# Setup of a fused condition-and-FFN kernel on one Trainium2 core: column sums on VectorE, a large write in four parts, two transfers shared with ScalarE, and a new order

## The reference

```python
# block 0
h   = gelu(gelu(cond @ W0 + b0) @ W1 + b1)
att = softmax(h @ W2 + b2)                      # 128 samples x 8
agg_w = einsum('bk,koi->boi', att, weight)      # one 64x64 matrix per sample
agg_b = att @ bias_k
c = einsum('boi,bih->boh', agg_w, x) + agg_b[:, :, None]
x = x + c @ (A @ B.T).T + bias                  # rank 128, 1024 -> 1024
# block 1
c = conv1d(x, w, K=9, pad=4, groups=4) + (cond @ c_weight.T)[:, :, None] + fside[None, :, None]
z = einsum('nh,erh->ner', c, lora_A); top1 = argmax(c @ gate_w.T + expert_bias)
x = x + c @ W_up.T + lora_B[top1] @ z[top1]     # 1024 -> 1024
```

## Time and profile before

| | us |
|---|---|
| median of 3 runs | 1119.54 |
| range of the runs | 1117.38 to 1119.77 |
| the profiled execution's own time | 1119.37 |
| its span | 1117.6 |
| TensorE busy | 1085.9 (97%) |
| VectorE busy | 911.1 (82%) |
| ScalarE busy | 613.5 (55%) |
| mean granted TensorE clock | 0.99 |

### The profile page before, as it was taken

How to read it: one execution, slowest core, us unless ns; L and a number is a source line. 1 busy time by engine, 2 the same in 40 slices (tenths; PEclk the granted TensorE clock), 3 DMA queues, 4 the chain that set the end, 5 groups by cost and what they waited for, 6 DMA issues and landing times.

```text
span 1117.6 us, 19137 instructions
## 1 busy us (share of the span) xinstructions
PE 1085.9 (97%) x7020; PEld 1052.2 (94%) x7020; DVE 911.1 (82%) x1670; ACT 613.5 (55%) x1243; POOL 4.5 (0%) x17
## 2 busy tenths in 40 slices
PE   6599999999999999999999999999999999999998
PEld 4478999999999999999999999999999999999998
DVE  5899788888878878878888887887887887888774
ACT  5675555545555555555655555554555555555541
POOL 1000000000000000000000000000000000000000
PEclk9699999999999999999999999999999999999999
DMA  8844455554445554445554454555445555544321
GB/s 317 268 71 135 117 119 151 149 141 138 116 106 153 143 159 128 122 120 128 146 153 138 137 119 104 154 146 151 132 118 114 142 144 156 132 136 121 83 58 76
DMA packets 118048, 152.03 MB, mean 136 GB/s; under 512 B 21836, under 2 KB 91980, under 8 KB 117804
## 3 DMA queue, kind: packets, MB, share of 16 engines
q1 hardware_dynamic: 116516, 148.49, 49.4%
q10 hardware_dynamic: 1440, 2.33, 0.6%
HBM read 80.87 MB, written 35.95 MB: 105 GB/s over the span
## 4 chain that ended last, share of the span: by engine, by line
PE 91%; DVE 4%; DMA 2%; issue 1%; SPq 1%; ACT 1%; DVEq 0%; ACTq 0%
PE M L1398 41%; PE H L1398 9%; PE G L1398 9%; PE F L1347 8%; PE F L1299 7%; PE F L1269 3%; PE F L1271 3%; PE F L1270 3%; PE F L1332 2%; PE M L1332 2%; PE M L1429 2%; DMA Br<-in_Bd_dram 1%; PE F L1287 1%; PE F L1286 1%; DMA Xr<-x 1%
## 5 line engine op out<-in xcount | busy, mean ns | idle before, releaser
L1398 PE MATMUL M<-Wsh,yh 128*128 128x384 f32 x896 | 313.1, 349 | 0.4 <-DVE yl L939 0.4
L1398 PE MATMUL M<-Wsh,yl 128*128 128x384 f32 x896 | 302.9, 338 | 0.0
L1398 PE MATMUL M<-Wsl,yh 128*128 128x384 f32 x896 | 302.9, 338 | 0.0
L888 DVE STREAM_TRANSPOSE yr<-F 128x512 f32<-128x512 f32 x126 | 90.2, 716 | 128.9 <-PE F L1347 80.7
L1398 PEld LDWEIGHTS M<-Wsh,yh 128*128 128x128 f32 x896 | 168.6, 188 | 5.6 <-DVE yl L939 0.7
L1398 PEld LDWEIGHTS M<-Wsl,yh 128*128 128x128 f32 x896 | 168.9, 188 | 2.8
L1398 PEld LDWEIGHTS M<-Wsh,yl 128*128 128x128 f32 x896 | 168.2, 188 | 0.0
L438 ACT ACTIVATE yh<-yr 128x1024 fp32r<-128x1024 f32 (+1 forms) x127 | 120.2, 946 | 53.6 <-DVE yr L903 41.4
L539 ACT ACTIVATE F<-F,cbX 128x128 f32<-128x128 f32 x248 | 69.0, 341 | 94.9 <-PE F L1332 94.1
L539 ACT ACTIVATE F<-M,cbX 128x128 f32<-128x128 f32 x260 | 72.4, 342 | 66.1 <-PE M L1332 66.0
L438 ACT ACTIVATE xTh<-xTr 128x1024 fp32r<-128x1024 f32 x64 | 67.3, 1052 | 61.7 <-DMA xTr<-in_xT_dram 61.7
(11 more groups left out here) (206 smaller groups left out, 2478.0 us busy)
## 6 DMA issues: line engine op xcount, KB each, us to landing
x<-in_xP_dram SPq DMA_DIRECT2D x64, 516.0 KB, 4.2
out_dram<-x SPq DMA_DIRECT2D x64, 516.0 KB, 3.5
xTr<-in_xT_dram SPq DMA_DIRECT2D x64, 512.0 KB, 4.0
Xr<-x SPq DMA_DIRECT2D x508, 64.5 KB, 2.5
agb<-agb_scratch SPq DMA_DIRECT2D x31, 128.0 KB, 3.5
agg_scratch<-stage SPq DMA_DIRECT2D x1, 2048.0 KB, 9.1
agg<-agg_scratch SPq DMA_DIRECT2D x60, 32.0 KB, 3.3
Wsr<-in_Wsd_dram SPq DMA_DIRECT2D x2, 768.0 KB, 11.0
```

Source lines behind the costliest of these rows:

```text
L888: dve.transpose(dst.rearrange("p j k m -> p (j k) m").rearrange("p (k r) (g b n) -> p g b k r n", r=2, g=2, b=4)[:, g % 2], F[g % 2][:, :] ...
L1398: last = pe.matmul(dst, w[:, y, k, :], m, start=fresh and n_ == 0, stop=k == 3 and n_ == 2, skip_group_check=True)
```

## The change

What it does, engine by engine:

- VectorE sums B over its eight blocks (`tensor_reduce` of 128x1024 to 128x128, into `bsums`), and one float32 matmul with ones replaces the 16 of `bsum`. `blo`, which overwrites `Br`, waits for it.
- `agg_out` becomes four writes of 512 KB. The first three are issued ahead of `load_x(0)`, the fourth between `load_agg1(1)` and `load_agg1(2)`. Readers wait for all four.
- ScalarE issues half of the second half's DMAs too (`rx1`), as it does in `rx0`, and makes the condition terms (`cb`), as activations.
- The written-out order of the setup and of the first steps changes on all four engines. The loops over `it` are unchanged, and so are the tiles' sizes and the arithmetic but for the column sums.

```diff
-            def agg_out():
+            def agg_out(c):
                 sp.wait_ge(v_ag, 2)
                 sp.wait_ge(a_ag, 6)
-                sp.dma_start(aggD.rearrange("n i o -> n (i o)"), stage[:, :]).then_inc(d_gw, 16)
+                sp.dma_start(aggD[:, 16 * c:16 * c + 16, :].rearrange("n i o -> n (i o)"), stage[:, 1024 * c:1024 * c + 1024]).then_inc(d_gw, 16)
...
+            def rx1():      # SP
+
+                sp.wait_ge(v_x1, 4)
+                for b in range(4):
+                    sp.dma_start(raw(0, 1)[:, b, :], x1[16 * b:16 * b + 16, 1, :, :]).then_inc(d_rx[1], 16)
...
+            def rx1():      # ScalarE
+                act.wait_ge(v_x1, 4)
+                for b in range(4):
+                    act.dma_start(raw(0, 1)[:, 4 + b, :], x1[64 + 16 * b:80 + 16 * b, 1, :, :]).then_inc(d_rx[1], 16)
...
+            def cb(g):      # ScalarE; the one of VectorE goes
+                act.wait_ge(d_fs, 16)
+                act.wait_ge(p_cb, 1)
+                act.activation(cbX[:, g, :], G[:, 128 * g:128 * g + 128], ACT.Identity, bias=fsB[:, g:g + 1]).then_inc(a_cb, 1)
...
+            def bsum():     # VectorE
+                dve.wait_ge(d_b, 16)
+                dve.wait_ge(p_mlp, 3)
+                dve.tensor_reduce(bsums, Br[:, :, :].rearrange("p c r -> p r c"), AX.X, ALU.add).then_inc(v_bs, 1)
...
             def bsum():     # TensorE
                 pe.wait_ge(a_ag, 2)
-                pe.wait_ge(a_b, 1)
                 pe.wait_ge(g_con, 6)
-                for c in range(8):
-                    pe.matmul(M[2][:, 64:66], Bh[:, c, :], onesr[:, 0:2], start=c == 0, stop=False)
-                pe.wait_ge(v_b, 1)
-                for c in range(8):
-                    last = pe.matmul(M[2][:, 64:66], Bl[:, c, :], onesr[:, 0:2], start=False, stop=c == 7)
-                last.then_inc(p_cs, 1)
+                pe.wait_ge(v_bs, 1)
+                pe.matmul(M[2][:, 64:66], bsums, ones[:, 0:2], start=True, stop=True).then_inc(p_cs, 1)
```

More of the change, by code:

```diff
@@ L132, in adaln_ffn @@
         h2 = small[:, 544:672]
+        bsums = small[:, 832:960]
         att = small[:, 672:680]
@@ L145, in adaln_ffn @@
         ccX = over("ccX", "yl", [128, NG, 8, 16], 1088)
-        onesr = over("onesr", "yl", [128, 128], 1600, f32r)
+        ones = over("ones", "yl", [128, 2], 1600)
         Xr2 = over("Xr2", "yl", [128, 8, 129], 1728)
@@ L428, in _ @@
             pool.tensor_copy(wkh[:, wkc(1)], wkr[:, wkc(1)]).then_inc(g_wk, 1)
[L429 removed]
+            pool.memset(ones[:, :], 1.0).then_inc(g_con, 1)
             for i in range(E):
@@ L696, in _ @@
             wc(0)
+            bias(0, 0)
             ah()
-            w11()
+            cb(0)
+            cb(1)
             ut(0)
-            bias(0, 0)
+            bias(0, 1)
             tuu(0)
-            bias(0, 1)
             txh(1, 0)
             vhi(0)
+            cb(2)
+            agb_out()
             txh(1, 1)
+            w11()
+            wc(1)
             bias(0, 2)
-            agb_out()
-            wc(1)
             bias(0, 3)
             rx0()
+            lora()
             th()
+            w21()
             ut(1)
-            bias(1, 0)
+            rx1()
+            xsr0()
             tuu(1)
-            bias(1, 1)
-            lora()
-            w(0)
-            xsr0()
-            w21()
             xsd(0, 0)
+            cb(3)
+            lh()
             pc(0, 0)
             pc(0, 1)
-            lh()
+            bias(1, 0)
+            vhi(1)
             xsr(0, 1)
-            vhi(1)
             xsd(0, 1)
-            w(1)
+            w(0)
+            bias(1, 1)
             hA(0)
             pc(0, 2)
-            w(2)
-            pc(0, 3)
+            w(1)
+            pc(0, 3)
+            w(2)
+            cpGH(0)
+            txh(2, 0)
             bias(1, 2)
@@ L1382, in row @@
                     pe.wait_ge(v_f, 6 * (s - 1) + 5)
+                if k == 0 and b == 7 and s == 0:
+                    pe.wait_ge(a_zt, 1)
                 if k == 0 and b == 9:
@@ L1490, in _ @@
             unit_o(0, 1)
+            unit_u(1, 0)
+            unit_u(1, 1)
             unit_o(0, 2)
-            unit_u(1, 0)
             unit_o(0, 3)
-            unit_u(1, 1)
             unit_tu(1)
             unit_p(0, 0)
+            unit_p(0, 1)
             unit_v(1)
-            unit_p(0, 1)
             unit_c(0, 0)
@@ L1501, in _ @@
             unit_o(1, 0)
+            unit_p(0, 2)
             unit_o(1, 1)
-            unit_p(0, 2)
+            unit_p(0, 3)
+            unit_c(0, 2)
             row(0, 0, 0)
             row(0, 0, 1)
-            unit_p(0, 3)
             row(0, 0, 2)
-            unit_c(0, 2)
             unit_c(0, 3)
             row(0, 0, 3)
+            row(0, 1, 0)
             unit_o(1, 2)
-            row(0, 1, 0)
             row(0, 1, 1)
-            unit_o(1, 3)
             row(0, 1, 2)
@@ L1518, in _ @@
             row(0, 2, 1)
+            unit_o(1, 3)
             row(0, 2, 2)
+            unit_u(2, 0)
             row(0, 2, 3)
-            unit_u(2, 0)
             row(0, 4, 0)
@@ L1526, in _ @@
             row(0, 3, 0)
+            unit_p(1, 0)
             row(0, 3, 1)
-            unit_p(1, 0)
             row(0, 3, 2)
+            unit_p(1, 1)
             row(0, 3, 3)
             unit_c(1, 0)
-            unit_p(1, 1)
             unit_u(2, 1)
+            row(0, 5, 0)
             unit_zt(0)
+            unit_c(1, 1)
             unit_tu(2)
-            unit_c(1, 1)
-            row(0, 5, 0)
-            unit_v(2)
             row(0, 5, 1)
             row(0, 5, 2)
+            unit_v(2)
             row(0, 5, 3)
-            unit_dl(0, 0)
             row(0, 6, 0)
             row(0, 6, 1)
-            unit_dl(0, 1)
             row(0, 6, 2)
@@ L1548, in _ @@
             row(0, 7, 0)
-            unit_o(2, 0)
-            unit_o(2, 1)
+            unit_dl(0, 0)
+            unit_dl(0, 1)
             row(0, 7, 1)
@@ L1553, in _ @@
             row(0, 7, 3)
+            unit_o(2, 0)
             row(0, 8, 0)
+            unit_dl(0, 2)
+            unit_o(2, 1)
             row(0, 8, 1)
```

137 lines of the change are left out of this document (66 added, 71 removed).

## The result

The changed kernel takes 1122.49 us (median of 16 runs, 1119.4 to 1124.67), the kernel before beside it 1118.8 (16 runs, 1117.19 to 1120.27). The ratio is 1.0029, with a 95% interval of 1.0022 to 1.0036: **slower**, by 0.3%, where 0.2% can be told. The forecast was 1116.8, and the range ended at 1121.0.

The account below looks back on a forecast made before the run. TensorE is gapless from 125 us, so only the start of work after its last large wait at 107.44 us counts. Gains of 1.6 + 0.7 + 0.3 = 2.6 us from 1119.37 give 1116.8 us; range 1113.8 to 1121.0.

Parts of the forecast that it names:

- Column sums: Start of setup: a 1.2 us reduction and one matmul replace 16 matmuls; `unit_u(0, 0)` comes 2.2 us earlier, near 20.7.
- `unit_v(0)`: Setup: waits for ScalarE's last small piece, released by a DMA; starts at 27.1 instead of 28.08, a 1.0 us gain.
- the 28 that I had named as a sign of being wrong: Setup: the forecast counts as wrong if `unit_v(0)` starts later than 28 us.
- `w12` and `t3`: Setup: `w12` lands at about 35, not 30.6; `t3` on VectorE waits 1.2 us, covered by later need.
- `rx0` and `rx1`: Setup: `rx0` starts at 32.75, ScalarE issues `rx1` in 4.88 us; first `unit_p` at about 46, not 45.10.
- the rival of two engines side by side: Setup DMA issue: ScalarE is free 2.3 us earlier, giving 1114.8 us; chance 0.24.
- `unit_o(1, 0)`: Setup: second half's 2.75 us data wait goes; starts at about 53.7, not 55.27, 1.6 us earlier.
- From there to 107.44: Rest of setup: 0.7 us net from small waits, despite about 1.4 us at row block 4, plus 0.3 from `unit_u(3, 0)`.
- The loop: From 125 us on: TensorE busy without a gap, order unchanged; the change is worth nothing there except by shifting its start.
- a difference of more than 1 us: Last wait to the end: the forecast counts as wrong if this time differs by more than 1 us.
- Small pieces held by the writes: Setup: early writes delay `unit_v(0)`; 1119.7 us if to 30.0, 1122.9 if to 33.2; chances 0.14 (about 30), 0.10 (past 32).
- Nothing that lasts: Start's gain lost to 1.4 us at row block 4 and late weight quarters; within 1 us of 1119.4; chance 0.10.

Follow-up runs that it names:

- experiment 3: The kernel before with only the column sums made by VectorE and one matmul: 1120.4 us, ratio 1.0012 to the kernel before.
- the second execution: One more profiled execution of the changed kernel, nothing altered: 1122.77 us by its own time.
- experiment 5: The changed kernel with `load_agb(1)` on SP put back behind `load_agg1(3)`: 1119.86 us, ratio 1.001 to the kernel before.
- experiment 9: The kernel before with only `rx1`, the second half's DMAs, shared by SP and ScalarE: 1117.56 us, ratio 0.9991.
- experiments 5 and 7: The latter: the kernel before with VectorE's column sums, 14 small added matmuls and the write in four parts, three early: 1118.89 us, ratio 1.0002.

## Why the prediction was wrong

- **Column sums.** The reduction took 1.87 us, between the 1.2 that I took and my bound of 2.4. `unit_u(0, 0)` came at 21.00, forecast near 20.7. Right in mechanism and nearly in size. But `unit_u(0, 0)` then took 4.48 us for its 24 matmuls, where it had taken 3.82: they start 0.21 us apart until 24.1 and 0.12 us apart after that, and before the change fewer of them fell into the slow part, which ended at 24.5. (The granted clock is recorded as 1.00 in both.) So 1.9 us at its start were 1.2 at its end. Alone, the sums are worth about 1.2 us of setup by the medians (experiment 3).
- **`unit_v(0)`.** Forecast 27.1, measured 27.13, but released by ScalarE's `u` and not by a DMA. The number is partly luck. The last piece landed at 26.98, near the forecast, and `u` was done 0.1 us after it. In the second execution it was 28.32, past the 28 that I had named as a sign of being wrong: there ScalarE began its first copy of `u` 1.6 us after `unit_u(0, 0)` had ended (0.3 us in the first). It was late since it needed 5.94 us, where it had needed 2.50, to issue the pieces. I priced the early writes by when data lands, and did not see that they make the *issuing* engines stand.
- **`w12` and `t3`.** Forecast: lands near 35, a wait of 1.2 us, covered. Measured: 35.87, a wait of 1.75. It was covered: the wait for `rx0`'s data behind it was longer.
- **`rx0` and `rx1`.** Here the first step failed. I put `rx0` on both engines at 32.75. ScalarE's came at 32.86 and SP's at 35.69, because `load_agb(1)` had been placed ahead of it on SP. That row stands in the order shown ahead of the prediction, and I did not ask what it waits for. `unit_p(0, 0)` came at 47.88, not 46. Taking that one row back gave 0.2% (experiment 5). ScalarE's issue of `rx1`, 5.37 us, was near the 4.88 taken; without the traffic it is 2.5 (experiment 9), so the rival of two engines side by side is right about the engines and wrong about this kernel's queue. (What I said for that rival was misread: the 2 MB write had been queued at 30.10, ahead of all eight DMAs of `rx0`, and not between the quick and the long ones.)
- **`unit_o(1, 0)`.** Forecast 53.7, measured 54.29 and 55.41, against 55.27 and 54.14 before: over two executions each, the gain of 1.6 us is not there. The second half's wait for `Xr` on VectorE is gone, as said, but the first half's, of 2.11 us, is new.
- **From there to 107.44.** I took 1.0 us in gains. There was none: the last wait ended at 107.44 and 109.09, against 107.44 and 106.41 before. The wait at row block 4 was there, with 0.87 us for the 1.4 forecast. What I had not seen is the 1.40 us at 62.80, once more a load on SP behind a wait, that of `load_agb(2)` for `vv(1)`.
- **The loop.** The step that failed most was the sentence that nothing the change does can be worth anything there, except by shifting its start. The loop's code is the same and it took 2.0 us longer. I had set a difference of more than 1 us as what would make the forecast wrong, and it is the larger part of the loss. Its cause, as far as the runs go, is the meeting of TensorE's instruction packets with the loads of the transposed `x`'s second half. In the sum this term stood at 0 and measured +2.0; the setup's terms stood at −2.6 and measured +1.3 by the profiles and +1.7 by the medians.
- **The rivals.** Small pieces held by the writes: in the changed kernel the last one landed 0.1 us ahead of need, and in experiments 5 and 7 `unit_v(0)` did wait for it; but what was late was its issue, and its flight was no longer than before. Nothing that lasts: this is the setup's story, but with other takers than I named.

What stays open: how a packet of 16 KB makes a load of 512 KB come 1 us late, and when. Of the second half's loads with a packet up to 0.5 us after the issue, 8 of 46 were late; with one at +0.8 to +2.0 us, 16 of 20. That the packets are TensorE's rests on their number and on the tests with added matmuls. No run changed the packets alone.

## What to carry to other kernels

When the order of a queue changes, ask of each row that moved ahead what it waits for, and add up what then stands behind it: here two such rows on SP ate more than the column sums gave. Judge a setup by many runs, or by two or three profiles: a single one was off by up to 2.4 us here. A part of the program whose code is unchanged can still change its time where a load has little slack (here 0.6 us between a landing after 3.6 us and a wait at 4.2); compare the time per step of the loop, before and after, ahead of any explanation. Give such a load more slack, or test with a few idle instructions whether the loop's time depends on them, before an edit upstream is judged by its total.
